# A decoder kernel's first wait and its last tail: constants moved behind the first evacuations, norms shared by two engines, the gate's product ahead of its tangent

## The reference

```python
x = _layernorm(x + _L0_attn_ref(x, ...))          # state-space mixer (1024 channels x 16 states) + FFN of 1408
x = _layernorm(x + _L0_xattn_ref(ctx_1024, x, ...)) # second mixer over the context, gated: y * silu(z), z = x
x = _layernorm(x + _L0_ffn_ref(x, ...))           # 8 experts, top 2, and a shared one
x = _layernorm(x + _L1_attn_ref(x, ...))          # segment attention against 16 fixed keys
x = _layernorm(x + _L1_xattn_ref(x, ctx_1024, ...)) # softmax(q k^T) over tokens, from the context
x = _layernorm(x + _L1_ffn_ref(x, ...))           # softmax router, top 8 biases
```

## Time and profile before

| | us |
|---|---|
| median of 3 runs | 3063.85 (3062.40 to 3065.66) |
| the profiled execution, its own time | 3062.09 |
| its span in the profile | 3060.3 |
| busy: PE / DVE / ACT / POOL | 2543.3 / 2422.9 / 1190.6 / 1053.4 |
| mean granted TensorE clock | 0.902 |

### The profile page before, as it was taken

The page is one execution under the profiler, slowest core; times in us unless marked ns, Lnnn a source line. Parts: engine busy times, 40 slices in busy tenths (PEclk is TensorE's granted clock), DMA queues, the critical chain, the costliest instruction groups (busy, mean ns, idle before and its releaser), DMA issues.

```text
span 3060.3 us, 21508 instructions
## 1 busy us (share of the span) xinstructions
PE 2543.3 (83%) x6908; PEld 1222.8 (40%) x6908; DVE 2422.9 (79%) x1788; ACT 1190.6 (39%) x1952; POOL 1053.4 (34%) x299
## 2 busy tenths in 40 slices
PE   4777989888979887789798785898787859999997
PEld 1234434333434443344344443343444424455554
DVE  5997898988989988899899998898999985121122
ACT  4334446444253452443433533433445432021222
POOL 1333343344434445424434454244443442001000
PEclk6886999998989998789889997899799879999999
DMA  4124426332212674022116650221155512216930
GB/s 134 33 79 162 139 105 199 103 105 100 65 38 88 221 239 142 26 101 64 42 67 206 222 175 20 95 83 48 66 183 184 183 44 69 76 45 208 296 110 14
DMA packets 160391, 350.14 MB, mean 114 GB/s; under 512 B 30680, under 2 KB 48088, under 8 KB 155608
## 3 DMA queue, kind: packets, MB, share of 16 engines
q1 hardware_dynamic: 134680, 271.89, 28.4%
q10 hardware_dynamic: 20480, 60.10, 5.2%
q0 software_dynamic: 5120, 16.78, 1.7%
HBM read 304.55 MB, written 61.73 MB: 120 GB/s over the span
## 4 chain that ended last, share of the span: by engine, by line
PE 40%; DVE 33%; issue 14%; ACT 5%; POOL 4%; DMA 3%; ACTq 0%; DVEq 0%; SPq 0%; POOLq 0%
DVE hb L1634 14%; PE ps L969 7%; PE ps L976 6%; DVE hb L1642 5%; PE ps L777 4%; DVE hb L1547 4%; PE ps L824 3%; PE ps L942 3%; PE ps L831 3%; POOL ya L1907 2%; DMA ring<-in_w_edn 2%; PE ps L1127 2%; PE ps L1012 2%; PE ps L899 1%; DVE sm L1496 1%
## 5 line engine op out<-in xcount | busy, mean ns | idle before, releaser
L1907 POOL TENSOR_TENSOR ya<-ya,hb 128x2048 f32<-128x2048 f32 x188 | 857.0, 4559 | 1318.9 <-DVE hb L1634 1007.2
L1634 DVE TENSOR_TENSOR_SCAN hb<-da,hb 128x2048 f32<-128x2048 f32 x192 | 856.2, 4459 | 1.5 <-ACT da L1175 0.2
L1175 ACT ACTIVATE da<-dl,pk 128x511 f32<-128x511 f32 x768 | 489.7, 711 | 423.1 <-DVE hb L1634 409.2
L1547 DVE TENSOR_TENSOR hb<-du,ps 128x2048 f32<-128x2048 f32 x192 | 435.8, 2270 | 33.4 <-POOL ya L1907 27.4
L1642 DVE TENSOR_TENSOR hb<-hb,ps 128x2048 f32<-128x2048 f32 x192 | 437.4, 2278 | 3.7 <-PE ps L916 2.9
L824 PE MATMUL ps<-V,ring 128*128 128x512 f32 x512 | 237.9, 616 | 22.0 <-DVE V L1575 9.1
L777 PE MATMUL ps<-ring,hid 128*128 128x512 f32 x544 | 245.7, 608 | 3.7 <-DVE hid L1679 3.7
L993 PE MATMUL ps<-ring,hid 128*128 128x352 f32 x480 | 197.0, 494 | 21.8 <-ACT hid L1404 15.6
L997 PE MATMUL ps<-ring,hid 128*128 128x352 f32 x480 | 192.0, 483 | 11.8 <-ACT X L1421 11.7
L1012 PE MATMUL ps<-ring,X 128*128 128x512 f32 x360 | 181.1, 639 | 12.9 <-DMA ring<-in_w_edn 12.1
L969 PE MATMUL ps<-T,ring 128*128 128x512 f32 x352 | 166.1, 616 | 17.4 <-DVE T L1667 17.4
(11 more groups left out here) (283 smaller groups left out, 3434.2 us busy)
## 6 DMA issues: line engine op xcount, KB each, us to landing
ring<-egu SPq DMA_DIRECT2D x240, 352.0 KB, 3.8
ring<-in_w_edn SPq DMA_DIRECT2D x72, 512.0 KB, 5.2
ring<-in_w_fgu SPq DMA_DIRECT2D x44, 512.0 KB, 3.6
hid<-xrows SPq DMA_DIRECT2D x60, 256.0 KB, 4.2
yrows<-X ACTq DMA_DIRECT2D x60, 256.0 KB, 4.6
ring<-wc SPq DMA_DIRECT2D x24, 512.0 KB, 4.1
ring<-in_w_egu SPq DMA_DIRECT2D x24, 512.0 KB, 3.5
ring<-in_w_edn SPq DMA_DIRECT2D x60, 192.0 KB, 4.1
```

What stands on the lines that cost most here:

```text
L1175: i = act.activation(dav(n % 2)[:, k, 1:], dl[:, k, 1:], ACT.Exp, scale=Aneg[:, (4 * (u % 3 - 1) if u % 3 else UC) + k, m:m + 1])
L1547: dve.tensor_tensor(hbv(m % NHB), du[:, :, :], wide(ps[:, 5, :], 4), ALU.mult).then_inc(s["dbu"], 1)
L1634: dve.tensor_tensor_scan(hb[:, h, :], da[:, b % 2, :], hb[:, h, :], 0.0, ALU.mult, ALU.add)\
L1907: pool.tensor_tensor(sums, ya[:, :, :], hbv(m % NHB), ALU.add).then_inc(s["acc"], 1)
```

## The change

1. VectorE's constants after `unit` become a task of the order, `consts`, between `c_bc` of sequence 0 and `dt_c` of unit 0. ScalarE waits for `unit` (`count` of 1) in place of `set`.
2. TensorE gets 20 fillers ahead of `c_bc` and 4 ahead of `dt_mm` of the first unit, after a wait for the pack of constants. All fillers now read the columns of the identity.
3. In the tail of the last sequence (`SHARE`), ScalarE makes the shifts and applications of tiles 0 and 2 and the evictions of 0 and 2; VectorE's new tasks `ln_d` and `ln_x` apply tiles 1 and 3 as (x + negated mean) * rstd and copy 1 and 3. Every reader there waits for all four tiles.
4. In all sequences the gate is computed as (0.5 * nat * yb) first, into `hid`, and then (T1 + 1) times that.
5. Eight groups of fillers are made smaller by 2 or 4.

```diff
-KEEP = [(("t_sq", 0), ("ffn_mm", 0), 6), (("res_t", 0), ("v_in", 0), 12), (("v_in", 0), ("gate", 0), 3),
-        (("gate", 0), ("ln_t", 1), 15), (("ln_t", 1), ("route_a", 0), 3), (("exp_down", 5), ("ln_t", 2), 16),
-        (("ln_t", 2), ("s_in", 0), 6), (("s_in", 1), ("seg_e", 0), 4), (("seg_e", 0), ("seg_t", 0), 2),
-        (("seg_t", 0), ("ln_t", 3), 8), (("xmix", 3), ("ln_t", 4), 12), (("ln_t", 4), ("bias_a", 0), 3),
+SHARE = (SEQS - 1,)
+BEGIN = {("c_bc", 0): 20, ("dt_mm", 0): 4}
+KEEP = [(("t_sq", 0), ("ffn_mm", 0), 6), (("res_t", 0), ("v_in", 0), 8), (("v_in", 0), ("gate", 0), 3),
+        (("gate", 0), ("ln_t", 1), 11), (("ln_t", 1), ("route_a", 0), 1), (("exp_down", 5), ("ln_t", 2), 12),
+        (("ln_t", 2), ("s_in", 0), 4), (("s_in", 1), ("seg_e", 0), 4), (("seg_e", 0), ("seg_t", 0), 2),
+        (("seg_t", 0), ("ln_t", 3), 4), (("xmix", 3), ("ln_t", 4), 8), (("ln_t", 4), ("bias_a", 0), 1),
         (("bias_a", 0), ("bias_b", 0), 9), (("bias_b", 0), ("bias_c", 0), 1)]
...
@@ plan()
+            put(20, ("consts", b, 0), "dve", 6.0, (("c_bc", b, 0), "dve"))
...
@@ tensor
+                def keep(count):
+                    for _ in range(count):
+                        pe.matmul(ps[:, 7, 0:2 * P], ones, pk[:, COL["ident"]:COL["ident"] + 2 * P], start=True, stop=True)
                 for t, b, n in order["pe"]:
+                    if b == 0 and (t, n) in BEGIN:
+                        pe.wait_ge(s["pk_in"], 16)
+                        keep(BEGIN[t, n])
...
-                            pe.wait_ge(*of("nrm", b, 4 * (n - 1) + (e + 1 if n == 2 else TT)))
+                            pe.wait_ge(*of("nrm", b, 4 * (n - 1) + (e + 1 if n == 2 and b not in SHARE else TT)))
...
-                            pe.wait_ge(*of("v", b, e + 1))
+                            pe.wait_ge(*of("v", b, TT if b in SHARE else e + 1))
...
-                            pe.wait_ge(*of("xe", b, 6))
+                            pe.wait_ge(*of("xe", b, 8 if b in SHARE else 6))
...
-                            pe.wait_ge(*of("xe", b, 8 + e + 1))
+                            pe.wait_ge(*of("xe", b, 12 if b in SHARE else 8 + e + 1))
@@ scalar
-                act.wait_ge(s["set"], 1)
+                act.wait_ge(s["count"], 1)
...
-                        tables()
+                        if before != ("dt_exp", b, 0):
+                            tables()
...
-                        for e in range(TT):
+                        mine = range(0, TT, 2) if b in SHARE else range(TT)
+                        for e in mine:
                             i = act.activation(shift[:, e:e + 1], mv[:, e, 0:1], ACT.Copy, scale=r4[:, e:e + 1])
...
-                        for k in range(KC):
+                        for k in range(0, KC, 2) if b in SHARE else range(KC):
                             act.activation(X[:, k, :], ps[:, k, :], ACT.Copy).then_inc(s["xe"], 1)
@@ vector
+                    elif t == "ln_d":
+                        dve.wait_ge(*of("rstd", b, (2, 3, 4, 6, 7)[n]))
+                        for e in range(1, TT, 2):
+                            dve.tensor_scalar(nat[:, e, :], (nat if n == 2 else ps)[:, e, :], mv[:, e, 0:1], r4[:, e:e + 1],
+                                              ALU.add, ALU.mult).then_inc(s["nrm" if n else "v"], 1)
+                    elif t == "ln_x":
+                        dve.wait_ge(*of("nat", b, n + 1))
+                        for k in range(1, KC, 2):
+                            dve.tensor_copy(X[:, k, :], ps[:, k, :]).then_inc(s["xe"], 1)
                     elif t == "gate":
                         dve.wait_ge(s["acc"], NST * (3 * b + 1))
                         for e in range(TT):
+                            dve.wait_ge(*of("v", b, TT if b in SHARE else e + 1))
+                            dve.scalar_tensor_tensor(out=hid[:, e, :], in0=nat[:, e, :], scalar=0.5, in1=yb(b)[:, e, :],
+                                                     op0=ALU.mult, op1=ALU.mult).then_inc(s["g1"], 1)
+                        for e in range(TT):
                             dve.wait_ge(*of("gz", b, e + 1))
-                            dve.scalar_tensor_tensor(out=T1[:, e, :], in0=T1[:, e, :], scalar=1.0, in1=nat[:, e, :],
-                                                     op0=ALU.add, op1=ALU.mult).then_inc(s["g1"], 1)
                             dve.wait_ge(*of("g1", b, e + 1))
-                            dve.scalar_tensor_tensor(out=T1[:, e, :], in0=T1[:, e, :], scalar=0.5, in1=yb(b)[:, e, :],
-                                                     op0=ALU.mult, op1=ALU.mult).then_inc(s["g2"], 1)
+                            dve.scalar_tensor_tensor(out=T1[:, e, :], in0=T1[:, e, :], scalar=1.0, in1=hid[:, e, :],
+                                                     op0=ALU.add, op1=ALU.mult).then_inc(s["g2"], 1)
```

53 lines of the change are left out of this document (31 added, 22 removed).

## The result

The changed kernel takes 3049.07 us (median of 6 runs, 3046.53 to 3053.59), the kernel before beside it 3064.76 (6 runs, 3062.40 to 3068.60): a ratio of 0.9949, 95% interval 0.9936 to 0.9962. That is 15.7 us less; the forecast was 22.5 (3041.4, range 3035 to 3050). Timed again beside the experiments, in one group 21 times, the kernel before took 3056.7 to 3069.4, median 3064.4. One execution of the kernel before, beside the last experiment, took 3811.4 us at a mean granted clock of 0.633 and is left out of every figure here.

The account below looks back on a forecast made before the run. A serial chain to 61 us, VectorE's scans to some 2560, then a tail with TensorE ahead bound the kernel. Start 13.5, gate 1.1 and tail 7.9 sum to 22.5 us: 3063.85 becomes 3041.4, range 3035 to 3050.

Parts of the forecast that it names:

- the gate of sequence 0: Gate of sequence 0: the product ahead of the tangent removes VectorE's 1.10 us wait; 1.1 us less, bounds 0 and 1.1.
- The 11.3 us from there to L880 are unchanged: Start: from ScalarE's first evacuation to L880 stays 11.3 us, VectorE having nothing new in between; L880 could start at 27.9.
- The clock of L880 and L899: Start: with fillers these TensorE products run at 2.4 GHz; L880 takes 3.70 us instead of 6.45.
- rival 3: Start gives only the wait, fillers not raising L880 and L899: 18 us in all, 3045.9; chance 0.12 together with Rival 4.
- The constants hidden: Start: constants moved into VectorE's idle time take at most 8.95 us, end 4.2 us before L1615, cost nothing.
- The distance at 2400 us: Sign of being wrong: the lead over the kernel before at 2400 us is not that of 61 us.
- rival 6: Scans make up the start's lost idle time by own waits: 9 to 13 of 13.5 us gone, 3053; chance 0.05.
- The tail, 7.9: Last tail: norm terms 1.7 + 2.4 + 1.7 - 0.3 + 2.4 = 7.9 us less, bounds 2 and 14.
- Rival 1: Last tail: joins cost nothing and the gate shows VectorE's full 3.8; tail 13.7, total 28.3 us, 3035.6; chance 0.08.
- Rival 4: Experts' weight transfers swallow the gain ahead of them: 4.1 us less, 3045.5; chance 0.12 together with rival 3.
- Rival 5: Start fillers run at 1.2 GHz, start gives nothing; with the tail also at the low level 14 us slower, 3078; chance 0.03.
- Rival 2: Clock falls in the tail's shortened stretches, costing 10 us: total 12.5, 3051.4; sign: slow transposes at norm 2; chance 0.12.

Follow-up runs that it names:

- e7: Changed kernel with GpSimd's eight diagonal products made to wait for VectorE's fourth silu; 3044.53 us.
- e2: Kernel before with the last tail's shared norms, joined waits and smaller filler groups alone, start and gate as before; 3059.45 us.
- e3: Changed kernel without its 20 and 4 fillers at the start; 3049.77 us.
- e1: Kernel before with the start's changes alone (constants moved, ScalarE's wait for unit only, start fillers); 3054.14 us.
- e6: Changed kernel with the last tail's filler groups cut to fit the waits, some behind norm 3's attention row; median 3046.4 us.
- e8: Changed kernel with the tail's filler groups of the kernel before (part 5 undone); one time, 3049.3 us.
- e9: Changed kernel with e7's GpSimd wait and e6's filler groups, plus more fillers around norm 4's transposes and ahead of bias_b; 3039.02 us.
- e4: Kernel before with part 4 alone, the gate's product with yb ahead of the tangent in all sequences; one time, 3063.1 us.
- e12: e9 with fillers around the folds alone: 6 ahead of the fourth c_mm, 5 ahead of the fifth fold, one ahead of each later fold; 3027.24 us.
- e5: Changed kernel with 56 more filler matmuls in TensorE's idle stretches from 42 to 210 us; 3045.90 us.
- e11: e9 with e5's fillers from 42 to 210 us and 16 more among the folds, from the fifth fold on; 3027.58 us.

## Why the prediction was right or wrong

The measured 3049.07 us lies inside the range of 3035 to 3050, but near its slow end, and partly by luck. In the trace the start gave 0.6 us less than forecast, the stretch behind it lost 5.3 that no term held, the tail gave 4.8 less, and the gate of sequence 0 gave 2.3 more: 14.0 us in place of 22.5. Without the gate's surprise the time would have been some 3051, outside the range.

- **ScalarE's wait**: right. 9.16 us at the first evacuation (9.0 forecast), with L1250's successor at 16.46.
- **"The 11.3 us from there to L880 are unchanged"**: wrong by 1.4 us. The constants had kept VectorE's silu pair out of GpSimd's way; moved forward, it met L1892 and took 2.84 in place of 1.47. e7 shows it. The forecast had even named GpSimd beside the constants, and didn't ask what the step moved to their place would meet.
- **The clock of L880 and L899**: as forecast in the trace (3.62 and 3.84), but its worth was measured against the long rows of a single trace. e2 has 5.22 and 4.66 with the old start. In the timed runs the fillers bring 0.7 us, less than can be told from nothing. The outcome is that of rival 3, though not its mechanism: the fillers do raise the level (e3 without them has 5.63 and 4.25), but what the start surely gives is the wait. Alone it measures 10.2 us.
- **The constants hidden**: right, with more air than thought: 2.3 us, not up to 8.95, as GpSimd was done by then.
- **The distance at 2400 us "not that of 61 us"**: this was named as the sign of being wrong, and it came. 5.0 us went by the twelfth scan and 0.3 more by the 61st. The cause isn't VectorE making up time (rival 6); it goes with where TensorE's slow rows fall in an execution. Eleven traces with the moved constants lost between -1.3 and 5.0 us there, the four with the changed kernel's own instructions (changed, e1, e6, e8) 5.0, 5.0, 1.3 and 1.4. Why an execution falls one way or the other stays open.
- **The gate of sequence 0**: mechanism right, size off: the term was 1.1 and measured 1.7, with 1.4 to 1.9 more behind it. The sum counted the wait at the gate and not the closer issue of the eight products, and put what follows in the tail of sequence 0 at nothing without a reason.
- **Gates of sequences 1 and 2: nothing**: right. The distance is 10.97 from the 120th scan to the 180th.
- **The tail, 7.9**: the terms were right and their condition wrong. They took the full clock for granted, on a row with 3.02 us of idle time and a fast product behind it. Filled as in e9, the tail gives 7.6 by the same terms. As changed it gave 3.1 in the profiled execution; the median of e2, without the gate, says 4.9. Norm 0 and the gate lost their 1.7 to v_in (5.40 for 3.70), norm 3 lost 1.6 to its transposes (3.58 for 1.97), and the routing 1.7 (its narrow products 5.96 for 5.09, L987 6.46 for 5.66). The 2.4 each of norms 1 and 4 came (2.5), and norm 2's 1.7 as well. With e6's fillers these two rows of the routing take 10.8 us together, as in the kernel before, and not the 12.4 of the changed one. The 1.7 of norm 0 and the gate counted the shared norm and part 4 together; e4 shows 2.0 from part 4 alone.
- **Rival 1** (3.8 us at norm 0 and the gate) didn't come in e9 either: TensorE's row of 3.73 us is the bound, as forecast. **Rival 4** didn't come: in e9 the distance to the kernel before is 17.5 us at the residual transposes, 21.7 ahead of the experts and 22.8 at s_in behind them. **Rival 5** neither: the granted clock from 20 to 36 us is 1.00.
- **Rival 2** was given 0.12, and it is what happened in the tail, at half its size. Its sign was badly chosen: slow transposes at norm 2 are in the trace (3.01 behind 3.20 us), but the kernel before has 2.77 there behind 1.15. It accounts for the 4.8 us that the tail is short of. By the medians, start and tail alone measure 10.2 and 4.9, and with the gate's 3.4 that would be 18.5, of which 15.7 were measured. The remaining 3 us are within the spread of the medians and stay open.

The forecast weighed a rule against that one row of 3.02 us and went by the row. The trace of the kernel before held the counterexample: norm 2's transposes, 2.77 us for 16 records behind a pause of 1.15, where norm 3's took 1.97 behind 0.93. The Trainium skill, "TensorE: Matmul & The Clock Gate", section "Part 1: The HAM clock gate", says that throttled is the default, and that the same kernel shows a different number of slow products from run to run; the runs here side with it on both (the first products of every trace run at the low level, and norm 3's transposes took 3.58 us in the changed kernel and 1.97 in e7, which has the same tail).

## What to carry to other kernels

A single row that shows a product fast after a pause is no licence to cut fillers: look for the shortest pause with a slow product behind it, in all the traces there are (here 1.13 us), and place fillers behind the last thing that TensorE must issue, not ahead of it. When a wait is removed, ask of each step that moves forward what runs on the neighbouring engines at its new time. And look for stretches where TensorE is busy all the time at a granted clock of one half: they hide from the busy share, and here one was worth 10.6 us in the traces and 11.8 by the medians (e12 against e9) against 15.7 for the whole change.

## What the runs showed of the hardware

- **Pauses and the clock.** L898 took 3.62 behind pauses of 1.34 to 1.56 us (changed kernel, e1, e7, e8) and 5.31 behind 2.19 and 2.51 (e5, e6), with the same instructions of TensorE ahead. At v_in and the transposes of norms 2 and 3 of the shared tail, pauses of 2.2 to 3.2 us were followed by slow products 14 times in 16 (changed kernel, e2, e3, e5, e7, e8), pauses of 0.5 to 1.5 us never in 17 (e6, e8 to e12). But in the three traces with the old tail (kernel before, e1, e4) norm 2's transposes took 2.77 to 2.78 us behind 1.13 to 1.15. With the two fast ones behind 2.22 and 3.20 us in e7, and the earlier trace rows, this says that a longer pause is a greater risk, not a rule, and that a pause alone doesn't decide.
- **Narrow products.** Among folds of eight records of 128x8 and two of 128x512 the granted clock stayed at 0.50 though TensorE was busy for 37.5 of 38 us; with one 128x256 filler to each fold, and a group of them ahead, it was 1.00 (e11, e12). Folds can run at the full level without fillers: the kernel before's at 205 us did (0.95 and 1.10), and in the changed kernel those from 257 us on, with two more wide records (L917) to each. The routing's 32 records of 128x8 are followed by slow L987 rows (5.4 to 6.5 us for 8 records) in every trace; fillers among these weren't tried.
- **Executions differ by where the low stretches fall.** Over 21 runs of the kernel before, the mean granted clock goes from 0.898 to 0.905 and the span from 3067.6 down to 3054.9, the two with a correlation of -0.80. The last 16 products alone took 8.5 us in eleven traces and 15.8 in three (e2, e6, e8).
- **VectorE beside GpSimd.** A 128x512 product with two inputs in SBUF takes 1.39 and 1.53 us beside GpSimd's, 0.68 and 0.69 alone. Small instructions suffer more: 128x16 0.17 alone and 1.01 beside it, 128x8 copies 0.08 and 0.29. The Trainium skill, "GPSIMD Engine Reference", section "1. Specifications", says that GpSimd shares its SBUF interfaces with VectorE and names instructions with two SBUF inputs; the traces agree (the convolutions, with one input in PSUM, take 4.54 for six in both). The slow 128x16 instruction and the copies have one SBUF input, so the two inputs aren't the whole story; no run here tests why.
